# Building the odd samples of the inverse row transform on GpSimd instead of VectorE

## The chip, the core and the metric

One core of a Trainium2 chip runs the whole program. Its engines run side by side, each with its own queue worked through in order: TensorE (PE, matmuls into the PSUM accumulators), VectorE (DVE), ScalarE (ACT), GpSimd (POOL) and SyncE (SP, here only the issue of transfers). They are kept in order by semaphores alone. The metric is the device time of one execution in microseconds (us).

## What is computed

An image batch x of 8 x 16 x 512 x 512 float32 values goes through four residual layers, each x = x + layer(groupnorm(x)). Only layer 1 is touched by the change:

```python
X = jnp.fft.rfftn(x, axes=(-2, -1), norm='backward')
...
Yr = _rconv(Xr, wr) - _rconv(Xi, wi) + b_real[:, None, None]
Yi = _rconv(Xr, wi) + _rconv(Xi, wr) + b_imag[:, None, None]
Y = lax.complex(Yr, Yi)
return jnp.fft.irfftn(Y, axes=(-2, -1), norm='backward')
```

A 3x3 convolution in the frequency domain: forward transform, convolution over the spectrum, inverse transform, and the sum onto x.

## The kernel before

The kernel works through the 8 images one after the other; layers 0 and 1 share a phase, layers 2 and 3 follow for all images in a second phase that the change leaves alone. In the first phase an image lies in SBUF as 64 tiles `X[:, j]` of 128 partitions (8 bands of rows x 16 channels) by 512 columns, held as two halves of 256. Layer 0 comes first. Layer 1 is then a software pipeline over 65 items i (an edge item 0 and one item for each tile, j = i - 1), in which every engine runs steps by hand-written order:

- ACT writes the normalised tile `xn` (L787, two steps ahead), POOL folds it into sums and differences for a half-length transform (`folded`, six operations L728 to L735, ends with `fold_ready`), and PE transposes the folded tile at the start of its step (L945), transforms it, mixes the channels (L981, L989) and transforms back into the accumulator `pZ` (L1000, L933). Between these, ACT and DVE copy accumulators to float16 as a high half (ACT) and a low half (DVE: `xt` L1118, `xh` L1127 and L1129, `yt` L1141).
- `pZ` holds 256 columns of even samples' sums and 256 columns of the odd samples: 128 cosine sums and 128 sine sums. ACT copies the latter to `zs` in SBUF (`odd_out`, L801, `zo_ready`). DVE then adds the even part to both halves of the tile (`even_part`, L1101, `z_free`), and makes from cosine and sine sums the 256 odd samples `zo` (L1104: 129 sums, L1105: 127 differences read backwards, `odd_ready`). POOL adds `zo` to one half of the tile and takes it off the other (`odd_part`, L742 and L743, `x2_ready`).
- `x2_ready` is waited for by the statistics of the finished tile on DVE (L1122) and ACT (L809), one step later, by SP for the store, and by ACT before it overwrites a `zs` buffer two items on.
- POOL's queue is: seven items folded ahead, then `odd_part(i)` and `folded(i + 6)` in turn, two pairs written out and 56 in a loop, then the last six odd parts. `xn`, `fold`, `zs` and `zo` have two buffers each.
- For images 0 to 6, every second step of PE from step 12 on also mixes a pair of tiles of the next image (`mix_pair`, L279), for which DVE finds maximum and minimum (L1053, L1058, one of them each step). ACT also works on the squares and sums (L816, L822) of the image after next, which images 6 and 7 don't have; the last image, number 7, has neither.

Of the kernel before, what the change touches and what calls it, by code (L numbers as in the profile page):

```python
# [20 lines left out]
J = H // BANDS  # L21
P = 128
ITEMS = J + 1
HALF = W // 2
NE = HALF // 2 + 1
NO = HALF // 2
# [125 lines left out]
def program(nc, x, w0, b0, w1r, w1i, b1r, b1i, w2, sw2, b2, w3, out):  # L152
    f32, f16 = mybir.dt.float32, mybir.dt.float16
    ALU = mybir.AluOpType
# [8 lines left out]
    with ctx:  # L163
        def sb(name, shape, dt=f32, c=ctx):
            return c.enter_context(nc.sbuf_tensor(name, shape, dt))
# [28 lines left out]
        with ExitStack() as p1:  # L194
# [351 lines left out]
            with ExitStack() as pm:  # L546
# [36 lines left out]
                zo = sb("zo", [P, 2, HALF], f32, pm)  # L583
                zs = sb("zs", [P, 2, HALF + 4], f32, pm)
# [10 lines left out]
                def s_(n):  # L595
                    return sem(n, pm)
# [13 lines left out]
                zo_ready, x2_ready, sq2_done, odd_ready = s_("zo_ready"), s_("x2_ready"), s_("sq2_done"), s_("odd_ready")  # L610
                z_done, z_free, edge_hi, edge_ready = s_("z_done"), s_("z_free"), s_("edge_hi"), s_("edge_ready")
# [96 lines left out]
                @block.gpsimd  # L708
                def _(pool):
                    nc.gpsimd.memset(dif[:, HALF:HALF + 1], 0.0)  # L710
                    nc.gpsimd.memset(zs[:, :, :], 0.0)
                    nc.gpsimd.memset(xh[:, :, :, :, :], 0.0).then_inc(pads_ready, 1)
                    pool.wait_ge(pads_ready, 1)
                    pool.sem_inc(dif_free, 1)

                    def root(b, n):
                        pool.wait_ge(var_ready, b * 3 + n + 1)
                        nc.gpsimd.tensor_tensor(rstd[:, :], var[:, 1:2], half_pow[:, :], ALU.pow).then_inc(rstd_done, 1)

                    def add_relu(b, j, k):  # L720

                        pool.wait_ge(leaky_done, b * J + j + 1)
                        nc.gpsimd.tensor_tensor(Xf[:, j], Xf[:, j], rl[:, k], ALU.add).then_inc(added_pool, 1)  # L723

                    def folded(b, i, k):
                        pool.wait_ge(xn_ready, b * ITEMS + i + 1)
                        pool.wait_ge(dif_free, b * ITEMS + i + 1)
                        nc.gpsimd.tensor_tensor(dif[:, 0:HALF], xn[:, k, 0:HALF], xn[:, k, HALF:W], ALU.subtract).then_inc(dif_done, 1)  # L728
                        nc.gpsimd.tensor_tensor(even[:, k], xn[:, k, 0:HALF], xn[:, k, HALF:W], ALU.add).then_inc(even_done, 1)
                        pool.wait_ge(dif_done, b * ITEMS + i + 1)  # L730
                        nc.gpsimd.tensor_tensor(fold[:, k, HALF:HALF + NO], dif[:, 0:NO], dif[:, HALF:NO:-1], ALU.subtract)
                        nc.gpsimd.tensor_tensor(fold[:, k, HALF + NO:W], dif[:, 1:NO + 1], dif[:, HALF - 1:NO - 1:-1], ALU.add).then_inc(dif_free, 1)
                        pool.wait_ge(even_done, b * ITEMS + i + 1)
                        nc.gpsimd.tensor_tensor(fold[:, k, 0:P], even[:, k, 0:P], even[:, k, P:HALF], ALU.add)
                        nc.gpsimd.tensor_tensor(fold[:, k, P:HALF], even[:, k, 0:P], even[:, k, P:HALF],  # L735
                                                ALU.subtract).then_inc(fold_ready, 1)

                    def odd_part(b, i, k):

                        j = i - 1  # L740
                        pool.wait_ge(odd_ready, b * J + i)
                        nc.gpsimd.tensor_tensor(X[:, j, 0], X[:, j, 0], zo[:, k], ALU.add)  # L742
                        nc.gpsimd.tensor_tensor(X[:, j, 1], X[:, j, 1], zo[:, k], ALU.subtract).then_inc(x2_ready, 1)  # L743

                    with pool.Fori(0, B) as b:
                        with pool.Fori(0, J // 4) as g:
                            for k in BY_POOL:
                                add_relu(b, g * 4 + k, k)
                        root(b, 1)
                        for i in range(7):  # L750
                            folded(b, i, i % 2)
                        for i in range(1, 3):
                            odd_part(b, i, i % 2)
                            folded(b, i + 6, i % 2)
                        root(b, 2)
                        with pool.Fori(1, (ITEMS - 7) // 2) as g:
                            for k in range(2):
                                odd_part(b, g * 2 + k + 1, (k + 1) % 2)
                                folded(b, g * 2 + k + 7, (k + 1) % 2)
                        for i in range(ITEMS - 6, ITEMS):  # L760
                            odd_part(b, i, i % 2)
                        root(b, 3)
# [285 lines left out]
                def _(dve):  # L1048
# [33 lines left out]
                    def even_part(link, b, u, k):  # L1082

                        if isinstance(u, int) and u == 0:

                            dve.wait_ge(edge_hi, b + 1)
                            nc.vector.tensor_scalar(es[:, 0:HALF], pZ[:, 0:HALF], R_SCALE / (EDGE_Y_SCALE * I_SCALE), k0e[:, :],
                                                    ALU.mult, ALU.add)
                            link(nc.vector.tensor_scalar(es[:, HALF:W], pZ[:, HALF:W], R_SCALE / (EDGE_Y_SCALE * I_SCALE), None,
                                                         ALU.mult))  # L1090
                            link(nc.vector.tensor_tensor(es, es, rhi[:, :], ALU.subtract))
                            link(nc.vector.tensor_scalar(es, es, lo_slot[:, :], None, ALU.mult))
                            nc.vector.scalar_tensor_tensor(out=edge_back[:, :], in0=rhi[:, :], scalar=hi_slot[:, :],
                                                           in1=es, op0=ALU.mult, op1=ALU.add).then_inc(z_free, 1)

                            dve.wait_ge(xn_ready, b * ITEMS + 2)
                            link(nc.vector.tensor_tensor(Xf[:, 0], Xf[:, 0], biasrow[:, :], ALU.add))
                        else:
                            j = u - 1
                            dve.wait_ge(zo_ready, b * J + u)  # L1100
                            nc.vector.scalar_tensor_tensor(out=X[:, j], in0=pZ[:, 0:HALF].unsqueeze(1).broadcast_to([P, 2, HALF]),  # L1101
                                                           scalar=1.0 / (Y_SCALE * I_SCALE), in1=X[:, j], op0=ALU.mult, op1=ALU.add,
                                                           accum_out=sum2[:, bass.ds(j, 1)]).then_inc(z_free, 1)
                            nc.vector.tensor_tensor(zo[:, k, 0:NO + 1], zs[:, k, 0:NO + 1], zs[:, k, NO + 1:HALF + 2], ALU.add)  # L1104
                            nc.vector.tensor_tensor(zo[:, k, NO + 1:HALF], zs[:, k, HALF:NO + 1:-1], zs[:, k, NO - 1:0:-1],  # L1105
                                                    ALU.subtract).then_inc(odd_ready, 1)

                    def step(link, b, i, k, on, p=None):
                        o = (k + 1) % 2
# [2 lines left out]
                        if on(4):  # L1112
                            even_part(link, b, i - 4, k)
# [689 lines left out]
```

## Time and profile before

| | us |
|---|---|
| median of 3 executions | 6232.46 (6221.11 to 6239.16) |
| the profiled execution | 6232.09 |
| its span, first to last instruction | 6230.2 |
| busy in it: PE, DVE, ACT, POOL | 5335.2, 5053.6, 4538.9, 3153.6 |
| POOL waiting for `zo` before L742 | 548.3, 496 times |
| POOL: L742 and L743 together | 745, 2 x 512 operations |
| DVE: L1104 and L1105 | 512 each, median 0.292 and 0.286 |

Busy time sums the durations of an engine's instructions; successive operations of an engine overlap a little, so what an operation costs its queue is the distance from its start to the next start, which is called its pitch below. Averages over the span mix two phases: the layer-1 pipelines of the eight images lie at about 440 to 777, 918 to 1255, 1396 to 1733, 1876 to 2212, 2358 to 2694, 2836 to 3172, 3314 to 3649 and 3792 to 4095 us.

### The profile page before, as it was taken

How to read it: one execution, taken by the hardware profiler on the slowest of the kernel's cores; microseconds unless marked ns; L12 is line 12 of the kernel's file. 1: busy time of each engine (PE TensorE's matmuls, PEld its weight loads, DVE VectorE, ACT ScalarE, POOL GpSimd, SP SyncE). 2: the span in 40 equal slices, each digit the busy share in tenths (PEclk: the TensorE clock that was granted, in tenths of full speed). 3: DMA queues.
4: the chain of work that ended last, by engine and by line, in shares of the span. 5: the costliest groups of instructions: out<-in, count | busy, mean ns of one | idle time of the engine just before them, and what ended most of it. 6: DMA issues, size and time to landing. Idle time of an engine off the chain costs nothing. (4 is left out here: it accounts for less than half of the span.)

```text
span 6230.2 us, 202732 instructions
## 1 busy us (share of the span) xinstructions
PE 5335.2 (86%) x63882; PEld 3402.6 (55%) x63882; DVE 5053.6 (81%) x10660; ACT 4538.9 (73%) x8793; POOL 3153.6 (51%) x5676
## 2 busy tenths in 40 slices
PE   0379979979979979979989989968898988989889
PEld 0058748748748748747757757833343433434334
DVE  5879979979979989988998998986676766767664
ACT  2578768868868867867876666768787877878775
POOL 3178768758858858858857858921111110111102
PEclk9889989989989989999999999989999999999999
DMA  6516616616616625625624524646676766767665
GB/s 203 158 47 209 204 40 206 207 46 201 206 53 190 208 69 171 208 88 159 206 95 115 159 84 113 177 94 155 166 204 163 204 162 159 200 162 196 168 163 139
DMA packets 535621, 958.88 MB, mean 154 GB/s; under 512 B 121946, under 2 KB 126938, under 8 KB 532826
## 3 DMA queue, kind: packets, MB, share of 16 engines
q1 hardware_dynamic: 467546, 798.95, 45.0%
q10 hardware_dynamic: 67456, 151.01, 7.8%
q8 instruction: 469, 7.68, 0.5%
q14 instruction: 150, 1.23, 0.1%
HBM read 560.40 MB, written 287.60 MB: 136 GB/s over the span
## 5 line engine op out<-in xcount | busy, mean ns | idle before, releaser
L1655 PE MATMUL pC<-xs,taps 128*128 128x512 f16 x4608 | 1095.8, 383 | 106.7 <-DMA xhalo<-xs 100.4
L981 PE MATMUL pM<-gw,xh 64*128 64x256 f16 (+1 forms) x24960 | 1130.7, 244 | 5.5 <-DVE yt L1141 4.7
L981 PEld LDWEIGHTS pM<-gw,xh 64*128 64x128 f16 x24960 | 972.5, 95 | 133.4 <-issue 12.0
L1551 POOL TENSOR_TENSOR xn<-xn,one_col 128x1 f32<-128x1 f32 x520 | 170.4, 328 | 1406.4 <-ACT xn L1585 1406.4
L1655 PEld LDWEIGHTS pC<-xs,taps 128*128 128x128 f16 x4608 | 449.3, 98 | 672.1 <-DVE xs L1705 90.2
L1571 ACT ACTIVATE scaled<-X,qbias,qscale 128x512 f32 (+1 forms) x512 | 413.3, 808 | 327.8 <-DMA X<-after_layer 297.0
L742 POOL TENSOR_TENSOR X<-X,zo 128x256 f32 (+1 forms) x512 | 372.5, 727 | 548.3 <-DVE zo L1105 548.3
L279 PE MATMUL pM<-X,mix0s 64*64 64x512 f32 x2304 | 530.1, 634 | 134.5 <-DVE X L1073 108.5
L723 POOL TENSOR_TENSOR X<-X,rl 128x512 f32 x384 | 478.4, 1275 | 270.8 <-ACT rl L772 270.7
L1593 ACT ACTIVATE xs<-xn 128x1028 f16<-128x1028 f32 x520 | 546.8, 1051 | 86.7 <-POOL xn L1552 86.2
L1712 DVE SCALAR_TENSOR_TENSOR result<-pC,X 128x512 f32<-128x512 f32 x512 | 352.4, 688 | 303.3 <-DMA out_dram<-result 181.4
L1642 PE MATMUL pC<-q,taps 128*128 128x512 f16 x1536 | 438.1, 395 | 142.6 <-DMA qhalo<-q 109.8
L1705 DVE TENSOR_TENSOR xs<-xn,xs 128x514 f16<-128x514 f32 x520 | 359.8, 692 | 229.0 <-ACT xs L1593 228.0
L832 ACT ACTIVATE xt<-pT 128x512 f16<-128x512 f32 x520 | 311.2, 598 | 258.7 <-PE pT L945 254.0
L279 PE MATMUL pP<-X,sumw 64*64 64x512 f32 x2048 | 465.7, 593 | 0.0
L772 ACT ACTIVATE rl<-pM,relu_b,relu_s 128x512 f32<-128x512 f32 x384 | 286.4, 778 | 227.4 <-DVE X L1067 214.7
L1118 DVE TENSOR_TENSOR xt<-pT,xt 128x512 f16<-128x512 f32 x520 | 356.2, 685 | 101.4 <-ACT xt L832 99.4
L1585 ACT ACTIVATE xn<-X,bs,rs 128x512 f32 (+1 forms) x520 | 417.9, 804 | 23.9 <-DVEq L1751 23.9
L933 PE MATMUL pZ<-inv_even,yt 128*128 128x256 f16 x3120 | 425.6, 273 | 0.0
L1657 PE MATMUL pC<-xhalo,halo 98*128 98x512 f16 x1536 | 417.4, 380 | 0.0
L787 ACT ACTIVATE rl<-X,bs,rs 128x512 f32 (+1 forms) x512 | 413.7, 808 | 0.0
L1141 DVE TENSOR_TENSOR yt<-pM,yt 128x512 f16<-128x512 f32 x520 | 354.9, 682 | 66.3 <-ACT yt L853 64.5
(249 smaller groups left out, 13574.2 us busy)
## 6 DMA issues: line engine op xcount, KB each, us to landing
gw<-row_weights SPq DMA_DIRECT2D x520, 288.0 KB, 3.4
after_layer<-X SPq DMA_DIRECT2D x512, 256.0 KB
out_dram<-result SPq DMA_DIRECT2D x512, 256.0 KB
X<-in_x_dram SPq DMA_DIRECT2D x448, 256.0 KB
X<-after_layer ACTq DMA_DIRECT2D x224, 512.0 KB, 5.7
stage<-in_x_dram SPq DMA_DIRECT2D x192, 512.0 KB
xhalo<-xs SPq DMA_DIRECT2D x504, 96.4 KB, 3.7
qhalo<-q SPq DMA_DIRECT2D x496, 96.2 KB, 3.9
```

The lines of the kernel that those rows point to most:

```text
L279: return nc.tensor.matmul(dst[c * HP:(c + 1) * HP], left, Xf[r * HP:(r + 1) * HP, j], start=start, stop=stop)
L723: nc.gpsimd.tensor_tensor(Xf[:, j], Xf[:, j], rl[:, k], ALU.add).then_inc(added_pool, 1)
L742: nc.gpsimd.tensor_tensor(X[:, j, 0], X[:, j, 0], zo[:, k], ALU.add)
L787: nc.scalar.activation(xn[:, k], Xf[:, u - 1], ACT.Identity, bias=bs1[:, :], scale=rs1[:, :]).then_inc(xn_ready, 1)
L933: m = nc.tensor.matmul(dst, left(p), right(q), start=first and n == 0, stop=last and n == 2)
L981: nc.tensor.matmul(pY[:, r, col:col + nd * P], row(xh, r)[:, k, p, ri, off:off + P], weights(r, q_, d, nd, ri), start=ri == 0 and off == 1 ...
L1571: nc.scalar.activation(scaled[:, k % 4], Xf[:, w], ACT.Identity, bias=qbias[:, bass.ds(b, 1)], scale=qscale[:, bass.ds(b, 1)]).then_inc(sc ...
L1585: nc.scalar.activation(xn[:, k % 2, 1:W + 1], Xf[:, tile], ACT.Identity, bias=bs3[:, :], scale=rs3[:, :]).then_inc(xn_ready, 1)
L1593: nc.scalar.activation(xs[:, 0:3:2, k], xn[:, (k - 1) % 2].unsqueeze(1).broadcast_to([P, 2, W + 2]), ACT.Copy).then_inc(hi_ready, 1)
L1642: nc.tensor.matmul(pC2[:, slot % 4], taps2[:, d], q[:, k, d:d + W], start=d == 0, stop=False)
L1655: nc.tensor.matmul(bank, taps3[:, d, wh], xs[:, h, own, d:d + W], start=d == 0 and n == 0, stop=False)
L1657: mm = nc.tensor.matmul(bank, halo3[:, d], xhalo[:, slot, d:d + W], start=False, stop=d == 2)
```

## The change

DVE's L1104 and L1105 go from `even_part` into POOL's `odd_part`, ahead of the two additions. POOL now waits for the copy of the sums (`zo_ready`, as DVE did), makes `zo`, waits for the even part (`z_free`, since DVE writes the same tile), then for its own result (`odd_ready`), and adds. The number of operations stays the same.

```diff
                     def odd_part(b, i, k):
 
                         j = i - 1
+                        pool.wait_ge(zo_ready, b * J + i)
+                        nc.gpsimd.tensor_tensor(zo[:, k, 0:NO + 1], zs[:, k, 0:NO + 1], zs[:, k, NO + 1:HALF + 2], ALU.add)
+                        nc.gpsimd.tensor_tensor(zo[:, k, NO + 1:HALF], zs[:, k, HALF:NO + 1:-1], zs[:, k, NO - 1:0:-1],
+                                                ALU.subtract).then_inc(odd_ready, 1)
+                        pool.wait_ge(z_free, b * ITEMS + i + 1)
                         pool.wait_ge(odd_ready, b * J + i)
                         nc.gpsimd.tensor_tensor(X[:, j, 0], X[:, j, 0], zo[:, k], ALU.add)
                         nc.gpsimd.tensor_tensor(X[:, j, 1], X[:, j, 1], zo[:, k], ALU.subtract).then_inc(x2_ready, 1)
...
                                                            accum_out=sum2[:, bass.ds(j, 1)]).then_inc(z_free, 1)
-                            nc.vector.tensor_tensor(zo[:, k, 0:NO + 1], zs[:, k, 0:NO + 1], zs[:, k, NO + 1:HALF + 2], ALU.add)
-                            nc.vector.tensor_tensor(zo[:, k, NO + 1:HALF], zs[:, k, HALF:NO + 1:-1], zs[:, k, NO - 1:0:-1],
-                                                    ALU.subtract).then_inc(odd_ready, 1)
```

## Rows read from the trace of the kernel before

**Rows 1.** Windows of images 7 and 1: length, busy (instructions) per engine, clock, DMA share, GB/s

```profile
3850.00:4060.00 210.00, 210.00 (x4105) 184.36 (x4103) 192.28 (x433) 152.54 (x347) 192.89 (x345) 1.00 0.67 178
...
1060.00:1250.00 190.00, 188.91 (x3445) 150.92 (x3442) 183.46 (x382) 152.06 (x342) 143.99 (x258) 1.00 0.64 206
```

**Rows 2.** Timeline of POOL, image 1: start, duration, instruction, idle before and releaser

```profile
1050.98 0.72 POOL L742 TENSOR_TENSOR X<-X,zo 128x256 f32 x1 [1.27 <-DVE zo L1105]
...
1054.54 0.46 POOL L734 TENSOR_TENSOR rl<-even 128x128 f32<-128x128 f32 x1
1054.96 0.46 POOL L735 TENSOR_TENSOR rl<-even 128x128 f32<-128x128 f32 x1
1056.17 0.73 POOL L742 TENSOR_TENSOR X<-X,zo 128x256 f32 x1 [0.75 <-DVE zo L1105]
```

**Rows 3.** Timeline, image 1: DVE's odd samples and what follows them

```profile
1022.97 0.29 DVE L1105 TENSOR_TENSOR zo<-zs 128x127 f32<-128x127 f32 x1
...
1023.41 0.69 DVE L1118 TENSOR_TENSOR xt<-pT,xt 128x512 f16<-128x512 f32 x1 [0.16 <-ACT xt L832]
1023.45 0.73 POOL L742 TENSOR_TENSOR X<-X,zo 128x256 f32 x1 [0.74 <-DVE zo L1105]
```

**Rows 4.** Timeline of PE, image 1: tile mixing (L279), then two step starts

```profile
1021.07 1.09 PE L279 MATMUL pP<-X,mix0s 64*64 64x512 f32 x8
...
1022.09 0.66 PE L945 MATMUL pT<-ident,rl 128*128 128x128 f32 x4
...
1027.01 0.60 PE L945 MATMUL pT<-ident,rl 128*128 128x128 f32 x4
```

**Rows 5.** Timeline of image 7: two step starts of PE, and POOL beside DVE

```profile
3901.95 0.60 PE L945 MATMUL pT<-ident,rl 128*128 128x128 f32 x4
...
3903.40 0.45 POOL L735 TENSOR_TENSOR rl<-even 128x128 f32<-128x128 f32 x1
...
3903.41 0.59 DVE L1104 TENSOR_TENSOR zo<-zs 128x129 f32<-128x129 f32 x1
...
3906.82 0.60 PE L945 MATMUL pT<-ident,rl 128*128 128x128 f32 x4
```

**Rows 6.** Timeline of POOL, setup of the second phase: one operation waits for the other

```profile
4121.81 0.09 POOL L1544 MEMSET one_col<- 128x1 f32 x1
4121.96 3.52 POOL L1546 MEMSET xhalo<- 2x4112 f16 x1
```

**Rows 7.** Timeline of image 2: before and at the first odd part, and the last transpose

```profile
1393.58 0.45 POOL L735 TENSOR_TENSOR rl<-even 128x128 f32<-128x128 f32 x1
...
1395.60 0.29 DVE L1105 TENSOR_TENSOR zo<-zs 128x127 f32<-128x127 f32 x1
...
1395.97 0.73 POOL L742 TENSOR_TENSOR X<-X,zo 128x256 f32<-128x256 f32 x1 [1.95 <-DVE zo L1105]
...
1713.53 0.60 PE L945 MATMUL pT<-ident,rl 128*128 128x128 f32 x4
```

**Rows 8.** The same in images 5 and 7, with the root operation L718 of image 7

```profile
2836.12 0.72 POOL L742 TENSOR_TENSOR X<-X,zo 128x256 f32<-128x256 f32 x1 [1.94 <-DVE zo L1105]
...
3152.10 0.60 PE L945 MATMUL pT<-ident,rl 128*128 128x128 f32 x4
...
3791.66 0.73 POOL L742 TENSOR_TENSOR X<-X,zo 128x256 f32<-128x256 f32 x1 [1.94 <-DVE zo L1105]
...
3800.93 0.67 POOL L718 TENSOR_TENSOR rstd<-var,half_pow 128x1 f32<-128x1 f32 x1
...
4077.27 0.60 PE L945 MATMUL pT<-ident,rl 128*128 128x128 f32 x4
```

**Rows 9.** Timeline of image 2's end: odd samples, minimum, next pair of tiles

```profile
1732.56 0.29 DVE L1104 TENSOR_TENSOR zo<-zs 128x129 f32<-128x129 f32 x1
...
1732.96 1.22 DVE L1058 TENSOR_REDUCE ymin<-pP 128x1 f32<-128x1024 f32 x1
...
1734.33 1.99 PE L279 MATMUL pP<-X,mix0s 64*64 64x512 f32 x8 [3.51 <-DVE ymin L1058]
```

## The prediction

> **What bounds the kernel now.** Read the windows first, one in the middle of image 1's pipeline and one in the last image's [rows 1]. PE is busy almost without a gap in both. In image 1 DVE is nearly as full (183.5 of 190 us) and POOL is not (144.0); in the last image POOL has 192.9 of 210. That already says that the two kinds of image will take the change differently, and that the page's average for POOL, about half of the span, is no guide to either.
>
> Next POOL's timeline, for how long one item occupies it. From L742 to L735 is 3.98 us without a gap [rows 2], and an operation on 128 columns costs its queue 0.42 (the pitch from L734 to L735), so an item is 4.39 to 4.40 us of POOL. Everything beyond is waiting: in image 1 the pair of items takes (1056.17 - 1023.45) / 3 = 10.91 us [rows 2, 3], 5.45 an item.
>
> Then PE, for its own floor. In the last image a step starts 4.87 after the one before [rows 5]. In image 1 mixing the pair of tiles takes 1022.09 - 1021.07 = 1.02 more in every second step [rows 4]. Two steps and a pair are 10.76, against 10.91 measured. The missing 0.15 is where PE runs behind DVE: DVE has only short waits, as at L1118 [rows 3]. So images 0 to 6 are bound by DVE and PE together, with DVE first by 0.15 in 10.91; the last image is bound by PE alone. Nowhere is POOL the bound.
>
> **What goes away.** On DVE, both operations together are 0.40 of pitch (1732.56 to 1732.96) [rows 9], more where they meet a POOL operation: L1104 took 0.59 in place of 0.29 beside L735 [rows 5]. DVE's load per item falls by 0.4 from about 5.26 (183.46 / 190 x 5.45) [rows 1], to well under PE's 5.38. What is late next is PE, so images 0 to 6 can win at most 0.15 a pair. PE mixes 26 pairs between steps 12 and 64: 26 x 0.15 = 4 us an image.
>
> The rows show that meeting as a doubled duration of DVE's operation. The Trainium skill has the reason (SBUF — State Buffer, section SBUF: two separate sides): a VectorE operation with two SBUF inputs and a GpSimd operation shut each other out for the whole instruction. This trace agrees. By that rule the cost of the meeting leaves with the two operations, since the other DVE operations of an ordinary item take at most one operand from SBUF; without the rule the sum is the same.
>
> **What is added on POOL.** Two operations on 129 and 127 columns, 0.83 us of pitch together, by the 128-column rows [rows 2]. L742 must then wait for POOL's own result. The operation lasts 0.46, and its successor would have started after 0.42 anyway; the next start comes 0.06 after the end, by the one place where POOL waits for itself (4121.90 to 4121.96) [rows 6]. That is 0.10 of stall. Inside the loop there is a surcharge: L742 starts 0.19 after L1105's end there [rows 3] and 0.08 after it in the code written out [rows 7], so 0.11 more. Bounds of the stall: 0.10 if the surcharge hides beneath the running operation, and 0.32 if a second wait on the way pays it too. I take 0.21, because L742 still needs its tile's address after the wait, as it does in [rows 3]. POOL's floor per item becomes 4.39 + 0.83 + 0.21 = 5.43 in the loop, 5.33 in the two written out.
>
> The other added waits are nothing. `zo_ready` comes from ACT's copy, before the even part: POOL no longer waits for DVE's L1101 and the two operations. `z_free` was implied before; L1101 starts beside POOL's `zo` and is shorter (0.6 against 0.83). Queued behind all waits on POOL are the folds, which PE needs; and L1122 on DVE and L809 on ACT, in order, wait for `x2_ready`. SP's stores do too, but the loads that they free are needed some three steps later. Nothing is moved past SP's queue.
>
> On the price, the Trainium skill (GPSIMD Engine Reference, section Elementwise — side-by-side cycle accounting) speaks against the move: GpSimd takes about 2.6 cycles per element where VectorE takes one, 1.96 times the time in its example. From DVE's 0.40 that would give an estimate of 0.78, and the sum about 0.05 an item lower; the rows for this very shape are used here.
>
> **The sum.** POOL will hardly ever wait from the first odd part on, so I add up its queue from there to the last fold, on which the last transpose (item 64) waits. In image 2 POOL can start `zo` when L735 is issued through, at 1394.0 (`zs` is there by then) [rows 7]. Then 0.67 for the root operation L718 [rows 8], 2 x 5.33 and 56 x 5.43: 0.67 + 10.66 + 304.1 gives 1709.4, and the transpose at 1709.5, which is 313.5 after the old first L742 at 1395.97. Before it was 1713.53 - 1395.97 = 317.6 [rows 7]: 4 us won. In image 5 it was 3152.10 - 2836.12 = 316.0 [rows 8]: 2.5 won. The seven images lie between 315.9 and 317.6, and give 3.2, 3.9, 4.0 (at PE's limit), 2.5, 3.1, 2.5 and 2.5, together -21.7.
> In the last image it was 4077.27 - 3791.66 = 285.6 [rows 8], because there PE keeps a step of 4.87 and POOL had room for it. With POOL at 5.43 it is also 313.5: +27.9.
> At the end of images 0 to 6 DVE is full, and PE waits for its minimum [rows 9]; two of the pairs of odd operations lie ahead of that, 2 x 0.40 a time: 7 x 0.8 = -5.6.
> Total: 27.9 - 21.7 - 5.6 = +0.6. From the profiled execution's 6232.1 that is 6232.7; the median of the runs shown is 6232.5, the same within 0.4 us.
>
> How steep it is matters more than the sum. POOL's loop has 56 items in 8 images, 448 in all: each 0.01 us on its floor is 4.5 us, as long as POOL is the bound. At a stall of 0.10 (5.33) the last image loses 22.3, the others are stopped by PE at -4.0 each, and with the ends the total is 22.3 - 28 - 5.6 = -11, 6221. At 5.47 the total is +18.7, which is 0.3% and about what a measurement of this kernel can tell from no change.
>
> **Rivals.** *The wait for its own result is dearer.* Place: between the second `zo` operation and L742. At a stall of 0.32, POOL's floor is 5.54, above the 5.45 of images 0 to 6: POOL, idle a fifth of the time there before, becomes the bound everywhere. Price 0.11 x 448 = 49: 6282. It decides from 5.47 on. For it: there are three waits in a row with computed values, and this trace has no POOL operation in a loop that waits for the one ahead of it. Against: the registers can be computed while `zo` runs.
> *Late additions stall DVE and ACT.* With POOL a step late, L1122 waits for `x2_ready` by some 0.5 us, at the same point in each item. DVE has gained 0.4 and POOL's pace allows as much again, so it should cost nothing; if it did, at 0.1 an item in 448, some +45: 6278.
> *PE's floor isn't a floor.* If PE's steps with a pair shrink once DVE is out of the way, and the stall is 0.10, the first seven images follow POOL at 5.33: each 5.6 quicker again than at 5.43, about 8.7 an image. 22.3 - 61 - 5.6 = -44: 6188. For it: PE's busy time is modelled. Against: 4.87 in the last image is without any wait for DVE, and it would have to hold there too.
> *The change doesn't do what it says*: POOL's new operations read backwards on both inputs and could cost more than the folds (which read one so). At 0.05 each it acts as the first rival: +45.
>
> **How the numbers follow.** The forecast, a floor of 5.39 to 5.47: 0.46. The cheap wait, 5.33 to 5.38: 0.13; both are within 0.3%. The dear wait and the dear operations: 0.29. Late additions: 0.05. PE without a floor: 0.07. So faster 0.07, same 0.59, slower 0.34. The predicted time is the forecast's, 6233. The range goes from a little under the cheap wait (6221), 6214, up to the dear wait, 6282; outside are the fast rival and the tail of the slow ones.
>
> **What would show it.** In the profile after: L742 starts 0.15 to 0.25 after the end of the second `zo` operation inside the loop, and 0.05 to 0.1 in code written out; POOL without idle time in both windows; items 5.38 to 5.47 apart in all eight images, the last one included, where they were 4.83 to 4.99; DVE busy less by about 0.5 an item, and waiting for POOL at L1122; PE waiting for L735 before its transposes. The first odd part to the last transpose is near 314 less the earlier start in every image. It is wrong if POOL still waits for `zo_ready`, if the last image stays under 5.2 an item, or if the distance in the loop is over 5.5.

## The result and the profile after

The changed kernel takes 6257.17 us (median of 7 runs, 6245.38 to 6272.22), the kernel before 6232.46 (7 runs). The ratio is 1.0043 with a 95% interval of 1.0026 to 1.0060: slower by 16 to 37 us, a change clear of the noise. The forecast was 6233, no change that a measurement could tell; the time lies 24 us above it, inside the stated range (6214 to 6282) but on its slow side.

| | before | after |
|---|---|---|
| profiled execution, us | 6232.09 | 6249.53 |
| its span | 6230.2 | 6247.7 |
| first odd part to last transpose, image 2 | 317.6 | 316.8 |
| the same, last image | 285.6 | 314.3 |
| last transpose to the last root operation L718, mean of images 0 to 6 | 27.7 | 26.8 |

The page's first part, busy time and share of each engine: 201 us have left DVE, 376 have come to POOL.

```profile
PE 5335.9 (85%) x63882; PEld 3397.4 (54%) x63882; DVE 4852.6 (78%) x9636; ACT 4532.8 (73%) x8793; POOL 3529.7 (56%) x6700
```

The same two windows as in [rows 1], now of the changed kernel:

```profile
1060.00:1250.00 190.00, 190.00 (x3435) 151.11 (x3435) 171.28 (x314) 152.52 (x345) 176.94 (x341) 1.00 0.65 207
3850.00:4060.00 210.00, 196.81 (x3671) 163.44 (x3670) 155.24 (x309) 141.29 (x310) 200.09 (x388) 1.00 0.59 160
```

In image 1 POOL has gone from 144 to 177 us and PE is full. In the last image PE is no longer full, and POOL has no gap but its wait for itself (0.25 an item, some 10 us in the window). POOL's timeline in image 1 (start, duration, instruction, idle before) answers [rows 2]; L742 and L743 now make the odd samples, L747 and L748 add them:

```profile
1042.83 0.48 POOL L735 TENSOR_TENSOR rl<-even 128x128 f32<-128x128 f32 x1
...
1043.25 0.43 POOL L742 TENSOR_TENSOR zo<-zs 128x129 f32<-128x129 f32 x1
...
1043.62 0.42 POOL L743 TENSOR_TENSOR zo<-zs 128x127 f32<-128x127 f32 x1
...
1044.29 0.72 POOL L747 TENSOR_TENSOR X<-X,zo 128x256 f32 x1 [0.25 <-POOL zo L743]
...
1049.72 0.73 POOL L747 TENSOR_TENSOR X<-X,zo 128x256 f32 x1 [0.25 <-POOL zo L743]
```

The distance is 5.43, to the hundredth what was forecast, and it stands at 5.43 in the loop of all eight images. The new operations have pitches of 0.37 and 0.36 us (the second is read in the kernel with the additions moved, below, where no wait follows it), and L747 starts 0.25 after the end of L743. That is POOL's wait for itself and not one for the even part: DVE had finished L1106 at least 1.1 us before, in every item of image 2's loop. PE in image 1, against [rows 4]:

```profile
1049.33 1.09 PE L279 MATMUL pP<-X,mix0s 64*64 64x512 f32 x8
...
1050.35 0.66 PE L950 MATMUL pT<-ident,rl 128*128 128x128 f32 x4
...
1055.27 0.60 PE L950 MATMUL pT<-ident,rl 128*128 128x128 f32 x4
```

The step is 4.92, as before; from 1225.84 to 1236.75 two steps and a pair take 10.91, as before. DVE's relief has won PE nothing. The last image, against [rows 5]:

```profile
3850.79 0.66 PE L950 MATMUL pT<-ident,rl 128*128 128x128 f32 x4 [0.33 <-POOL rl L735]
...
3853.26 0.69 DVE L1124 TENSOR_REDUCE tmax<-X  x1 [0.45 <-POOL X L748]
...
3856.22 0.66 PE L950 MATMUL pT<-ident,rl 128*128 128x128 f32 x4 [0.34 <-POOL rl L735]
```

PE's step was 4.87 and is 5.43, each waiting for POOL's fold. The ends of the pipelines, against [rows 7, 8], images 2 and 7:

```profile
1402.47 0.73 POOL L747 TENSOR_TENSOR X<-X,zo 128x256 f32<-128x256 f32 x1 [0.80 <-DVE X L1106]
...
1716.66 0.46 POOL L735 TENSOR_TENSOR rl<-even 128x128 f32<-128x128 f32 x1
...
1719.23 0.60 PE L950 MATMUL pT<-ident,rl 128*128 128x128 f32 x4
...
3791.59 0.72 POOL L747 TENSOR_TENSOR X<-X,zo 128x256 f32<-128x256 f32 x1 [0.80 <-DVE X L1106]
...
4105.89 0.66 PE L950 MATMUL pT<-ident,rl 128*128 128x128 f32 x4 [0.34 <-POOL rl L735]
```

In image 2 the last transpose comes 2.1 us after the last fold has ended (1717.1) and does not wait for it; in images 0 to 6 that room is 1.8 to 3.0 us. Measured from the first fold, the last transpose comes 345.2 us later before the change and 345.1 after it, as means of images 0 to 6. So the change costs 28.7 us in the last image and gives 0.9 at each of the seven ends: 28.7 - 6.1 = 22.6, near the measured 24.7. In this one profiled execution the setup phase was 6.4 us longer and the second phase 11 us shorter; neither is touched by the change, and the start of the first fold scattered from 407.3 to 419.5 us over the profiled executions of the kernels below.

### The profile page after: what moved, and what is told of

It reads as the page before. It is cut to its first block and busy times, and to the rows that moved or that the text cites. A ratio compares the mean times of both kernels' runs of the same rounds, so it can differ in the third digit from the quotient of the medians.

```text
span 6247.7 us, 203740 instructions
## 1 busy us (share of the span) xinstructions
PE 5335.9 (85%) x63882; PEld 3397.4 (54%) x63882; DVE 4852.6 (78%) x9636; ACT 4532.8 (73%) x8793; POOL 3529.7 (56%) x6700
## 5 line engine op out<-in xcount | busy, mean ns | idle before, releaser
L279 PE MATMUL pM<-X,mix0s 64*64 64x512 f32 x2304 | 531.5, 635 | 135.5 <-DVE X L1078 108.8
L279 PE MATMUL pP<-X,sumw 64*64 64x512 f32 x2048 | 465.8, 593 | 0.0
L747 POOL TENSOR_TENSOR X<-X,zo 128x256 f32 (+1 forms) x512 | 372.5, 727 | 129.1 <-POOL zo L743 113.4
L950 PE MATMUL pT<-ident,rl 128*128 128x128 f32 x2080 | 338.6, 287 | 96.6 <-POOL rl L735 94.3
```

The source lines that it names most:

```text
L279: return nc.tensor.matmul(dst[c * HP:(c + 1) * HP], left, Xf[r * HP:(r + 1) * HP, j], start=start, stop=stop)
```

## The experiments

**The loss is in the last image.** The first kernel undoes the change there, the second makes it there alone.

```diff
-                    with pool.Fori(0, B) as b:
+                    def whole_image(b, here):
...
+                    with pool.Fori(0, B - 1) as b:
+                        whole_image(b, True)
+                    whole_image(B - 1, False)
...
+                            if not b < B - 1:
+                                nc.vector.tensor_tensor(zo[:, k, 0:NO + 1], ...
```

> Undoes the change in the last image alone: images 0 to 6 make the odd samples on GpSimd, image 7 on VectorE. Theory (the whole loss is the last image, where POOL's 5.43 us an item replaces PE's 4.87; the first seven images neither win nor lose in the pipeline, and win 0.8 us each at their end): the last image's first odd part to last transpose is back at 285.6, the time is that of the kernel before less about 6, 6227, ratio 0.999. Rival (the first seven images carry part of the loss, by POOL being full or by a longer start): the time stays 5 to 15 us above the kernel before.

> The complement: images 0 to 6 make the odd samples on VectorE, image 7 on GpSimd. Theory: the last image's pipeline grows by 28 us, nothing else moves: 6260, ratio 1.0045. Rival (loss spread over all images): less than 20 us above the kernel before.

Measured: 6222.4 against 6227.1 us, ratio 0.9996 (0.9982 to 1.0010), for the change in images 0 to 6 alone; 6250.2 against 6227.1, ratio 1.0029 (1.0015 to 1.0043), for the change in image 7 alone. By the second interval that change costs 9 to 27 us. In the first, the last image runs from its first odd part to its last transpose in 285.6 us again:

```profile
3784.25 0.73 POOL L748 TENSOR_TENSOR X<-X,zo 128x256 f32<-128x256 f32 x1 [1.94 <-DVE zo L1116]
...
4069.86 0.60 PE L955 MATMUL pT<-ident,rl 128*128 128x128 f32 x4
```

In the second it takes 313.8, 28.2 more than before, just above what the interval allows. All of the loss that can be measured is there; in the other seven images the change can't be told from nothing, although the ends are 0.6 us shorter each in the profile.

**Is PE's floor 10.76 or 10.91?** The first kernel leaves out the odd samples altogether, the second relieves DVE by more than the change does, with the maximum of the next image's tiles over 8 columns in place of 1024.

```diff
-                        pool.wait_ge(zo_ready, b * J + i)
-                        nc.gpsimd.tensor_tensor(zo[:, k, 0:NO + 1], ...
-                        nc.gpsimd.tensor_tensor(zo[:, k, NO + 1:HALF], ...
...
-                        nc.vector.tensor_reduce(ymax[:, bass.ds(p, 1)], pair, AX, ALU.max)
+                        nc.vector.tensor_reduce(ymax[:, bass.ds(p, 1)], pair[:, 0:8], AX, ALU.max)
```

> Leaves the odd samples out altogether: neither VectorE nor GpSimd makes them, GpSimd adds what lies in the buffer. VectorE is relieved by 0.4 us an item as in the changed kernel, GpSimd has only its old work. As predicted (PE's floor for two steps and a pair is 10.76, and VectorE costs the other 0.15): the pipeline of images 0 to 6 shortens by 4 us each, with the ends 34 us in all, 6198. Rival (PE itself needs 10.91, VectorE's relief is worth nothing there): two steps stay at 10.91, the last transpose stays 345 us behind the first fold, only the ends win, 6226, ratio 0.999. The last image stays at 285.6 either way.

> The kernel before with the maximum over the next image's pair of tiles (1.13 us of VectorE in every second step) taken over 8 columns only, which leaves out most of that maximum: VectorE is relieved by 1 us in two steps, more than the change relieves it. As predicted at first (VectorE costs 0.15 in 10.91): two steps and a pair fall to 10.76. Rival (PE itself needs 10.91): they stay at 10.91, the first fold to the last transpose stays at 345 us.

Measured: without odd samples 6223.2 against 6227.1 us, ratio 0.9994 (0.9979 to 1.0009). With the short maximum, a single run, 6195.7; its gain is not in the pipeline but behind it, where DVE and PE alternate over the last pairs: the images follow each other 4.3 us closer. PE's transposes and pairs in both, the odd samples left out first:

```profile
1062.84 0.66 PE L945 MATMUL pT<-ident,rl 128*128 128x128 f32 x4
...
1073.74 0.66 PE L945 MATMUL pT<-ident,rl 128*128 128x128 f32 x4
```

```profile
1063.32 0.66 PE L945 MATMUL pT<-ident,rl 128*128 128x128 f32 x4
...
1074.22 0.66 PE L945 MATMUL pT<-ident,rl 128*128 128x128 f32 x4
```

Both 10.90. The last transpose lies 345.1 us behind the first fold in the first kernel (mean of seven), and within 0.3 us of that in the second. DVE's load is not what sets the 10.91, and PE is busy for 190.00 of 190 us after the change: PE needs it by itself. Where the 0.15 is shows in PE's rows after the change, the last inverse matmuls before an ordinary step, then before a pair:

```profile
1208.30 0.82 PE L938 MATMUL pZ<-inv_even,yt 128*128 128x256 f16 x6
...
1208.95 0.60 PE L950 MATMUL pT<-ident,rl 128*128 128x128 f32 x4
...
1209.39 0.50 PE L938 MATMUL pM<-fwd_odd,xt 128*128 128x128 f16 x6
...
1213.17 0.82 PE L938 MATMUL pZ<-inv_even,yt 128*128 128x256 f16 x6
...
1213.92 1.09 PE L279 MATMUL pP<-X,mix0s 64*64 64x512 f32 x8
...
1214.94 0.66 PE L950 MATMUL pT<-ident,rl 128*128 128x128 f32 x4
...
1215.43 0.50 PE L938 MATMUL pM<-fwd_odd,xt 128*128 128x128 f16 x6
```

From start to start, the same six matmuls hold PE 0.65 us before the transposes and 0.75 before the pair; the transposes take 0.44 after those matmuls and 0.49 after the pair. A pair costs PE its 1.02 and 0.15 at its two edges.

**Is the 0.25 before the addition POOL's wait for itself?** The additions move behind the first two operations of the next fold.

```diff
-                        pool.wait_ge(z_free, b * ITEMS + i + 1)
...
                         nc.gpsimd.tensor_tensor(even[:, k], xn[:, k, 0:HALF], xn[:, k, HALF:W], ALU.add).then_inc(even_done, 1)
+                        if late is not None:
+                            add_odd(b, late, k)
                         pool.wait_ge(dif_done, b * ITEMS + i + 1)
```

> GpSimd makes the odd samples as in the changed kernel, but does the first two operations of the next fold before it adds them, so that nothing waits for the operation just ahead. Theory (the 0.21 us between the second odd operation and the addition is a wait of GpSimd for itself): the distance in the loop falls from 5.43 to 5.22, the last image's pipeline from 313.9 to about 301.5, the other images keep PE's pace: 6243 to 6245, 12 us less than the changed kernel. Rival (it is a cost of issuing eight operations with their waits, wherever they stand): 5.43 stays, and the time with it.

Measured: 6258.3 against 6227.1 us, ratio 1.0055 (1.0039 to 1.0071). That is no faster than the changed kernel, where 12 us less were expected. Yet the theory holds for what it was about: the distance in the last image is 5.13, 0.30 less, and nothing on POOL waits there.

```profile
3851.31 0.73 POOL L752 TENSOR_TENSOR X<-X,zo 128x256 f32 x1
...
3856.44 0.73 POOL L752 TENSOR_TENSOR X<-X,zo 128x256 f32 x1
```

The last image lasts 13.8 us longer than in the kernel before, against 28.5 with the change as it was. But images 0 to 6 are each 3.2 us longer (mean) up to the last transpose. The place is one instruction of DVE, early in each image:

```profile
2385.95 4.29 DVE L258 TENSOR_TENSOR rm<-rstd,gm 128x1 f32<-128x1 f32 x1
...
2389.47 0.75 POOL L729 TENSOR_TENSOR even<-rl 128x256 f32<-128x256 f32 x1
...
2391.97 0.72 POOL L752 TENSOR_TENSOR X<-X,zo 128x256 f32 x1 [1.75 <-DVE X L1112]
```

A product of one column, 0.16 us elsewhere, lasts 4.29 us, from 2385.95 to 2390.24. POOL runs from before it to 2390.22 without a gap, and stops there only because its next operation needs DVE's even part (L1112), which stands in DVE's queue behind the product. PE then waits 2.65 us for the same even part.

**Is it shut out by GpSimd?** If so, another form of the same product should not be.

```diff
-                link(nc.vector.tensor_tensor(rm[:, :], rstd[:, :], gm[:, 0:1], ALU.mult))
+                link(nc.vector.tensor_scalar(rm[:, :], gm[:, 0:1], rstd[:, :], None, ALU.mult))
```

> As e4_wait_filled, but the small product of reciprocal deviation and mean (one column, L258), which took 4.3 to 4.6 us there in place of 0.16 while GpSimd ran without a gap, takes one tensor and one scalar operand in place of two tensors. Theory (it was shut out by GpSimd because both its inputs are tensors in SBUF): it takes 0.15 us, nothing takes its place, the first seven images lose their 3.5 us each again: some 24 us less than e4_wait_filled, 6233 to 6238, the last image stays 13 to 14 us longer than in the kernel before. Rival 1 (the 128-column product L264 after it, on tensor inputs of float32, is shut out in its stead): the stall moves there, the time stays near 6258. Rival 2 (the stall comes from the later additions, not from a shut-out): L258 stays long or the 3.5 us an image stay elsewhere.

Measured: 6255.1 against 6232.3 us, ratio 1.0037 (1.0022 to 1.0052); the profile has the last transpose 3.1 us late in images 0 to 6 still, so the 24 us expected back did not come. Both instructions over the whole trace (duration min/median/max in ns):

```profile
L258 DVE TENSOR_SCALAR rm<-gm,rstd x25: 203/214/215, 208.0 to 4130.2; 128x1 f32<-128x1 f32 x25
...
L264 DVE TENSOR_SCALAR mix0s<-mix,rstd x9: 286/3723/4070, 208.6 to 3825.6; 128x128 f32<-128x128 f32 x9
```

L258 takes 0.21 us now, and L264, 128 columns of float32 from one tensor, has taken the stall over: 3.7 us in place of 0.29. This is rival 1. It speaks for the shut-out: L258 ran at its usual time while POOL had no gap, so the stall goes with the form of the instruction, and L264 again ended only when POOL came to its wait for the even part. That nothing would take L258's place was wrong.

**How near the edge is POOL in the first seven images?** One more small operation an item.

```diff
                         nc.gpsimd.tensor_tensor(X[:, j, 1], X[:, j, 1], zo[:, k], ALU.subtract).then_inc(x2_ready, 1)
+                        nc.gpsimd.tensor_tensor(spare[:, k:k + 1], half_pow[:, :], half_pow[:, :], ALU.mult)
```

> The changed kernel with one more GpSimd operation per item, a product of one column into a spare tile after the additions. With d its pitch, 0.18 to 0.3 us: theory (at 5.43 GpSimd stands 2 us behind PE's needs at the last transpose of images 0 to 6, and is already the bound in the last): the distance becomes 5.43 + d in all eight images; images 0 to 6 grow by 58 d - 2 each, the last by 58 d. With d = 0.2: 7 x 9.6 + 11.6 = 79 us, 6336; with 0.3: 119 us, 6376. Rival (GpSimd has real room in the first seven images, because the others can wait for it): only the last image grows, 12 to 17 us, 6270.

Measured: 6303.2 against 6232.3 us, ratio 1.0123 (1.0108 to 1.0138).

```profile
1061.30 0.19 POOL L750 TENSOR_TENSOR spare<-half_pow 128x1 f32<-128x1 f32 x1
1061.45 0.73 POOL L729 TENSOR_TENSOR dif<-rl 128x256 f32<-128x256 f32 x1
```

The pitch is 0.15, less than the 0.18 assumed at least, and the distance 5.57 in the loop of all eight images, 0.14 more than after the change. The last transpose of images 0 to 6 now comes 5.4 us later than after the change, where 58 x 0.14 - 2 = 6.1 was due, and 7.1 later in the last one, where 8.1 was due. The sum 7 x 5.4 + 7.1 = 45 us stands against 46 by the medians (6303.2 - 6257.2, beside which the kernel before took 6232.3 and 6232.5). So 0.14 us more on POOL costs 46 us, since it takes POOL past PE's pace of 5.45; the rival, with room in the first seven images, is out.

## Why the prediction was right, and where not

- *POOL's floor, 5.43.* Right as a sum by luck: two errors cancel. The two operations cost 0.73 and not 0.83, and the stall 0.31 (0.67 from L743 to L747, less the 0.36 of its pitch) and not 0.21. The stall is 0.25 from end to start where [rows 6] have 0.06 and [rows 3] 0.19, so even the larger row was too small; filling the wait took 0.30 away (5.43 to 5.13). With this stall and the 0.83 of the forecast the floor would have been 5.53, the forecast's own dear wait.
- *The last image, +27.9.* Right: +28.7 by the same two events, and +23 us between the medians (9 to 27 by the interval) in the experiment that has the change there alone.
- *Images 0 to 6, -21.7.* Wrong, and this is the term that missed: it was 0, and it is nearly the whole of the 24 us between forecast and measurement. The failed step is "The missing 0.15 is where PE runs behind DVE". The floor of 10.76 was put together from an ordinary step of the last image and the pair's own time, and left out the 0.15 at the pair's edges. The other sign was there in [rows 1]: PE busy 188.9 of 190 us in image 1. With that term at 0 the prediction's own sum is 27.9 - 5.6 = +22.3, and the forecast would have been 6254.
- *The ends, -5.6.* About right: -0.9 for each of seven images, -6.1. In a difference of medians it can't be told from nothing by itself.
- *Late additions.* DVE does wait for them, 0.45 us an item in the last image and not at all in images 0 to 6, and PE did not lose by it: its steps are 5.43, POOL's own distance.
- *`zo` starts at once.* For the first item of an image not: L747 waits 0.80 us for the even part, so the additions start no earlier than before, and the last fold of image 2 ends 314.6 us after the first of them, not 313.5. Images 0 to 6 had the room for it.
- *The dear wait decides from 5.47 on.* The mechanism was right (0.14 more cost 46 us). As an estimate, the room of 1.8 to 3.0 us at the last transpose, spread over 58 items, puts the edge 0.03 to 0.05 above 5.43, near the 5.47 stated. The total at that floor is 0.6 + 0.04 x 448 = 18.5, not 18.7.

Of the signs that the text named, these came as written: 5.38 to 5.47 between items in the loop of all images, no idle POOL there but its own wait (0.25, at the end of the range given), PE waiting for L735 in the last image. These did not: in images 0 to 6 PE doesn't wait for L735 and DVE doesn't wait for POOL at its statistics, and the last transpose comes near 317 us after the first odd part, not 314; in code written out the wait is 0.14, not 0.05 to 0.1; DVE is relieved by 0.39 us an item (201 us over 512), not 0.5. None of its signs of being wrong came, for none of them looked at PE's pace in images 0 to 6, which is where the sum failed.

The time alone would not have told this: 6257 lies between the forecast and the dear wait, and neither of the two makes it. It comes from the forecast's floor with a term of -21.7 that isn't there.

Not settled: why the two new operations, one of them with two backward inputs, have pitches of 0.37 and 0.36 where those of the fold with as many columns have 0.42. No kernel here varied it.

## What to carry to other kernels

Moving work off a full engine wins only if that engine is what the pace hangs on: before counting a gain, add up the bound engine's own period where it does this very sequence of operations, edges between them included, and not from parts of another stage. Judge the engine that takes the work in the stage where it is fullest; here a share of 51% over the span hid 92% in the last image, which alone cost 28 us. Where one image or stage lacks the load that covers a move, keep the old form there, and keep in mind that an engine brought to within 0.02 us of the pace has no room left: here the next 0.14 us an item cost 46 us.

## What the runs showed of the hardware

A VectorE operation can be kept out for as long as GpSimd has no gap, not only for the length of one GpSimd operation. The product of one column (two tensor inputs) took up to 4.62 us, the 128-column float32 product of one tensor and one scalar 3.7 to 4.1, each over eight to ten GpSimd operations in a row; a one-column product with a scalar operand took 0.21 and a copy of one column 0.15 while GpSimd ran without a gap too. Both kernels have such a stall in each of the eight images. All sixteen ended within 0.1 us of the start of GpSimd's next gap, and that gap came only because GpSimd itself had to wait for VectorE's next result. GpSimd's short wait for itself in the changed kernel, 0.25 us an item, is such a gap: there L258 took 0.67 at most. Taking that wait away, by itself 0.30 us an item better, brought the stall. The Trainium skill (SBUF — State Buffer, section SBUF: two separate sides) names two kinds of VectorE operation, with two SBUF inputs or in a two-port mode, as shut out by GpSimd for the whole instruction. The trace agrees for the product of two tensors; whether L264 ran in a two-port mode no run here shows. In both the wait went over several GpSimd instructions.

A GpSimd operation that waits for the one ahead of it, in a loop with computed waits, starts 0.25 us after its end; for a pitch of 0.36 that makes 0.67. In code written out it starts 0.14 after the end, where nothing else holds it.
